# Row tiles in the plain aggregation runs: some gathers move from GpSimd to row-by-row DMAs of SyncE and ScalarE

## The reference

```python
h = layernorm(x + L0(x))       # messages (x @ weight[type])[src], summed by dst
h = layernorm(h + L1(h))       # mean of h[src] by dst, two 256x256 products, batch norm, relu
h = layernorm(h + L2(h))       # three attention layers: softmax by dst over the edges
h = layernorm(h + L3(h))       # (h @ W)[src] with degree norms, summed by dst
```

## Time and profile before

| | us |
|---|---|
| median of 3 runs | 6722.3 (6719.2 to 6724.4) |
| the profiled execution | 6704.8 |
| its span | 6703.0 |
| layer 0, to the first gather of a0 | 384.0 |
| POOL busy in the span | 4662.0 (70%) |
| PE busy | 4849.3 (72%) |
| DVE busy | 4466.5 (67%) |
| ACT busy | 2887.0 (43%) |

### The profile page before, as it was taken

The page is one execution under the profiler, slowest core; times in us unless marked ns, Lnnn a source line. Parts: engine busy times, 40 slices in busy tenths (PEclk is TensorE's granted clock), DMA queues, the critical chain, the costliest instruction groups (busy, mean ns, idle before and its releaser), DMA issues. The chain is left out here.

```text
span 6703.0 us, 99334 instructions
## 1 busy us (share of the span) xinstructions
PE 4849.3 (72%) x16858; PEld 2865.5 (43%) x16858; DVE 4466.5 (67%) x11760; ACT 2887.0 (43%) x11591; POOL 4662.0 (70%) x4938
## 2 busy tenths in 40 slices
PE   9977777777777757777675777775766777676666
PEld 4445555543444434444443444443444444333333
DVE  5145555555555578888886888886888888555554
ACT  3310000000000057888875888885788887000000
POOL 0057777767777727777776777777777777677776
PEclk9988778777777777878787888887787888767777
DMA  6444444433333345555544555555555553333333
GB/s 207 159 132 119 119 119 119 118 106 106 106 106 106 105 135 143 142 144 142 143 125 124 145 141 143 145 140 150 137 141 144 142 141 107 108 112 112 112 112 105
DMA packets 421891, 864.51 MB, mean 129 GB/s; under 512 B 103949, under 2 KB 246310, under 8 KB 421290
## 3 DMA queue, kind: packets, MB, share of 16 engines
q0 software_dynamic: 231040, 636.59, 34.6%
q1 hardware_dynamic: 151344, 184.21, 8.4%
q10 hardware_dynamic: 38906, 37.37, 1.8%
HBM read 755.70 MB, written 102.08 MB: 128 GB/s over the span
## 5 line engine op out<-in xcount | busy, mean ns | idle before, releaser
L631 POOL DMA_INDIRECT rows_a<-table,rows_src x2454 | 2348.8, 957 | 882.9 <-issue 527.3
L785 PE MATMUL ps<-rows_a,hot_a 128*128 x4980 | 1964.8, 513 | 749.6 <-DMA rows_a<-table,rows_tile_a 311.3
L1958 ACT ACTIVATE rows_a<-rows_a,ex_a 128x64 f32<-128x64 f32 x9588 | 2321.1, 337 | 0.0
L2035 PE MATMUL ps<-rows_a,hot_a 128*128 128x260 f32 x4908 | 1815.1, 490 | 161.0 <-DVE agg L1867 147.4
L729 DVE TENSOR_TENSOR agg<-agg,ps 128x256 f32 (+1 forms) x2490 | 1043.8, 419 | 1288.1 <-PE ps L785 1244.8
L686 POOL DMA_INDIRECT rows_a<-table,rows_tile_a x1500 | 1419.4, 946 | 456.9 <-issue 242.8
L785 PEld LDWEIGHTS ps<-rows_a,hot_a 128*128 128x128 f32 x4980 | 1059.2, 244 | 1574.8 <-DVE agg L729 824.7
L1867 DVE TENSOR_TENSOR agg<-agg,ps 128x260 f32 x2490 | 1037.6, 417 | 318.9 <-PE ps L2035 131.6
L2035 PEld LDWEIGHTS ps<-rows_a,hot_a 128*128 128x128 f32 x4908 | 973.7, 230 | 451.1 <-issue 346.3
L686 POOL DMA_INDIRECT rows_a<-table,row x782 | 742.3, 949 | 238.4 <-issue 140.0
L2125 ACT ACTIVATE root_a<-mv_a,eps 128x1 f32<-128x1 f32 x49 | 14.4, 295 | 973.5 <-DVE mv_a L2148 973.5
(11 more groups left out here) (341 smaller groups left out, 4223.8 us busy)
## 6 DMA issues: line engine op xcount, KB each, us to landing
dstt_a<-dloc_dram SPq DMA_DIRECT2D x156, 512.0 KB
own_a<-table SPq DMA_DIRECT2D x4608, 1.0 KB
table<-ob SPq DMA_DIRECT2D x48, 1024.0 KB, 4.4
rows_a<-table,rows_src POOLq DMA_INDIRECT x2454, 2.8
rows_a<-table,rows_tile_a POOLq DMA_INDIRECT x1500, 2.8
table<-ob_n SPq DMA_DIRECT2D x98, 130.0 KB, 2.8
rows_a<-table,row POOLq DMA_INDIRECT x782, 2.8
x_dram<-cur ACTq DMA_DIRECT2D x1, 6400.0 KB
```

Source lines behind the costliest of these rows:

```text
L631: nc.gpsimd.indirect_dma_start(out=rows[:, n % ring, 0:width], out_offset=None, in_=table, in_offset=bass.IndirectOffsetOnAxis(ap=index[:, ...
L785: nc.tensor.matmul(ps[n % banks][:, 0:width], hot[:, m % nbuf, j, :], mine[n % 4], start=True, stop=True).then_inc(step_done, 1)
L1958: ins = nc.scalar.mul(a, a, ex[:, k % GV, s, h:h + 1])
L2035: nc.tensor.matmul(ps[j % banks][:, 0:W4], hot[:, j, :], step_rows(k, j), start=True, stop=True).then_inc(step_done, 1)
```

## The change

Of the 782 tiles of each plain run, 29 are "row tiles", which POOL leaves out. Every 44th (43, 87, ... 747: 17 tiles) is fetched by SP row by row, 128 DMAs of 1024 bytes, with the row addresses loaded 32 at a time. Every 66th from 54 on (54, 120, ... 780: 12 tiles) is fetched by ACT in bursts of 16 rows: four bursts before its first block, then one inside each block's list and one behind it. The ring has 59 places instead of 64, and behind it lie three places for SP's tiles and two for ACT's, 64 in all. Layer 0 makes the places of these tiles and two lists of their row addresses, and stores the lists; SP loads a tile's list of 128 addresses before it or ACT asks for the rows. `AfterA1.act` and `AfterA5.act` get `between` behind their root in the same way as `AfterA0.act`.

```diff
-TRING = 64
+TRING = 59
 LOAD = 32
+OWN_TILE = 44
+OWN_TILES = tuple(range(OWN_TILE - 1, T - 1, OWN_TILE))
+OWN_PLACES = 3
+ACT_TILE = 66
+ACT_FIRST = 54
+ACT_TILES = tuple(range(ACT_FIRST, T - 1, ACT_TILE))
+ACT_PLACES = 2
+BURST = 16
+BURSTS_AHEAD = 4
...
@@ layer 0, SP behind L341 @@
+                        for q in range(2):
+                            sp.dma_start(own_tile_dram[q], own_tile[:, q]).then_inc(whole_out, 16)
@@ layer 0, DVE behind L449 @@
+                def own_place(stride, at, places, first):
+                    quotient(groups_of, tile, stride)
+                    ch.link(nc.vector.scalar_tensor_tensor(out=mine[:], in0=groups_of[:], scalar=float(-stride), in1=tile[:],
+                                                           op0=ALU.mult, op1=ALU.add))
...
+                own_place(OWN_TILE, OWN_TILE - 1, OWN_PLACES, TRING)
+                own_place(ACT_TILE, ACT_FIRST, ACT_PLACES, TRING + OWN_PLACES)
@@ aggregate, POOL @@
                 for t in range(T):
+                    if t in ROW_TILES:
+                        continue
@@ aggregate, SP @@
+                ask_index_of_act(0)
+                ask_index(0)
+                ask_index_of_act(1)
+                ready = 2
+                for i in range(len(OWN_TILES)):
+                    if i + 1 < len(OWN_TILES):
+                        ask_index(i + 1)
+                    if ready < len(ACT_TILES) and i == (ACT_TILE * ready - ACT_FIRST) // OWN_TILE:
+                        ask_index_of_act(ready)
+                        ready += 1
+                    if i >= OWN_PLACES:
+                        sp.wait_ge(step_done, min(OWN_TILES[i - OWN_PLACES] + NB, S))
+                    sp.wait_ge(own_in[i % 2], 16 * (i // 2 + 1))
+                    ask_rows(sp, mybir.EngineType.SP, own_index[:, i % 2], 0, P, LOAD, octets, 4 * D, table.shape[0] - 1,
+                             rows[:, TRING + i % OWN_PLACES, 0:D], own_full[i % OWN_PLACES])
@@ aggregate, ACT @@
+                def burst(done):
+                    q = next(bursts, None)
+                    if q is None:
+                        return
+                    i, lane = q * BURST // P, q * BURST % P
+                    place = i % ACT_PLACES
+                    if lane == 0:
+                        act.wait_ge(act_in[i % 2], 16 * (i // 2 + 1))
...
+                    ask_rows(act, mybir.EngineType.Activation, act_index[:, i % 2], lane, lane + BURST, BURST, octets, 4 * D,
+                             table.shape[0] - 1, rows[:, TRING + OWN_PLACES + place, 0:D], act_full[place])
+                    act.sem_inc(asked, 1)
+                for _ in range(BURSTS_AHEAD):
+                    burst(0)
                 for i in range(NB):
-                    after.act(act, i)
+                    after.act(act, i, lambda: burst(done_by(i)))
+                    burst(done_by(i))
@@ AfterA0.act @@
                 act.wait_ge(self.mixed, i + 1)
                 self.load_x(act, i + 2)
+            between()
             act.wait_ge(self.turned, i + 1)
```

More of the change, by code:

```diff
@@ L49 @@
 FW = 2 * P + 2
-TRING = 64
+TRING = 59
 LOAD = 32
+OWN_TILE = 44
[7 more added lines that the diff above has]
+BURSTS_AHEAD = 4
+assert not set(OWN_TILES) & set(ACT_TILES)
+ROW_TILES = (*OWN_TILES, *ACT_TILES)
+PLACES = OWN_PLACES + ACT_PLACES
 OWN_BATCH = 4
@@ L219, in steps_and_first_table @@
         odd = sb("odd", [P, SC], FP, c)
+        groups_of, mine, place = (sb(q, [P, SC], FP, c) for q in ("groups_of", "mine", "place"))
         joins = sb("joins", [P, 2, P], FP, c)
@@ L521, in _ @@
                                         4.0 * W4, None, ALU.mult)
+                for q, a in enumerate((row0, rows_tile)):
+                    for tiles, stride, lo in ((OWN_TILES, OWN_TILE, 0), (ACT_TILES, ACT_TILE, len(OWN_TILES))):
+                        n, at = len(tiles), tiles[0]
+                        each = a[:, 0:n * stride].rearrange("p (i e) -> p i e", e=stride)
+                        nc.vector.tensor_scalar(own_tile[:, q, lo:lo + n], each[:, :, at:at + 1].rearrange("p i e -> p (i e)"),
+                                                4.0 * D, None, ALU.mult)
                 nc.vector.tensor_copy(cont[:], crow.rearrange("o (k u) -> o u k", u=UG)[:, 0])
@@ L640, in build @@
     why_row = "row numbers are made from src and etype as the gathers' are"
-    why_slot = "slots are numbers modulo TRING"
+    why_slot = "slots are numbers modulo TRING, or one of the places behind the ring"
     def ask_rows(eng, of, numbers, lo, hi, load, flat, size, last, place, full):
@@ L645, in ask_rows @@
             _, at = nc.values_load_multi_w_load_instructions(
-                numbers[:, lane:lane + load], engines=[of], min_val=0, max_val=last * size,
+                numbers[:, lane:min(lane + load, hi)], engines=[of], min_val=0, max_val=last * size,
                 skip_runtime_bounds_check_because=why_row)
@@ L663, in aggregate @@
         width = D + 1 if with_deg else D
-        rows = sb(f"rows_{name}", [P, TRING, width], FP, c)
+        rows = sb(f"rows_{name}", [P, TRING + PLACES, width], FP, c)
+        own_index = sb(f"own_index_{name}", [1, 2, P], I32, c)
+        octets = table.bitcast(BYTE).rearrange("r b -> (r b)")
+        own_in = [sem(f"own_in_{name}{u}") for u in range(2)]
+        own_full = [sem(f"own_full_{name}{u}") for u in range(OWN_PLACES)]
+        act_index = sb(f"act_index_{name}", [1, 2, P], I32, c)
+        act_in = [sem(f"act_in_{name}{u}") for u in range(2)]
+        act_full = [sem(f"act_full_{name}{u}") for u in range(ACT_PLACES)]
+        asked = sem(f"asked_{name}")
         hot = sb(f"hot_{name}", [P, nbuf, u8, P], FP, c)
@@ L670, in aggregate @@
         for j in range(TRING):
-            used[j] += len(range(j, T, TRING))
+            used[j] += sum(1 for t in range(j, T, TRING) if t not in ROW_TILES)
         count = ps[7][:, 0:P]
@@ L697, in _, with ask_index, ask_index_of_act @@
                 after.sp_first(sp)
+                def ask_index(i):
+                    sp.dma_start(own_index[:, i % 2], own_tile_dram[0 if with_deg else 1, :, i:i + 1].rearrange("p o -> o p"),
+                                 allow_slow_non_contiguous=True).then_inc(own_in[i % 2], 16)
+                def ask_index_of_act(i):
+                    if i >= 2:
+                        sp.wait_ge(asked, P // BURST * (i - 1))
+                    at = len(OWN_TILES) + i
+                    sp.dma_start(act_index[:, i % 2], own_tile_dram[0 if with_deg else 1, :, at:at + 1].rearrange("p o -> o p"),
+                                 allow_slow_non_contiguous=True).then_inc(act_in[i % 2], 16)
+                ask_index_of_act(0)
[13 more added lines that the diff above has]
+                             rows[:, TRING + i % OWN_PLACES, 0:D], own_full[i % OWN_PLACES])
+                assert ready == len(ACT_TILES)
             @block.vector
@@ L747, in _ @@
                 after.act_first(act)
+                bursts = iter(range(len(ACT_TILES) * P // BURST))
+                def burst(done):
[6 more added lines that the diff above has]
+                        act.wait_ge(act_in[i % 2], 16 * (i // 2 + 1))
+                        if i >= ACT_PLACES:
+                            free = ACT_TILES[i - ACT_PLACES] + NB
+                            assert free <= done
+                            act.wait_ge(step_done, free)
+                    ask_rows(act, mybir.EngineType.Activation, act_index[:, i % 2], lane, lane + BURST, BURST, octets, 4 * D,
[3 more added lines that the diff above has]
+                    burst(0)
                 for i in range(NB):
-                    after.act(act, i)
+                    after.act(act, i, lambda: burst(done_by(i)))
+                    burst(done_by(i))
                 after.act_last(act)
+                assert next(bursts, None) is None
             @block.tensor
@@ L767, in rows_of @@
                     return views
-                landed, ahead = 0, rows_of(0)
+                landed, ahead, turns = 0, rows_of(0), list(base)
                 for m in range(UNITS):
@@ L781, in _ @@
                         while landed <= tile_by(n):
-                            u, turn = landed % TRING, landed // TRING
-                            pe.wait_ge(slot_full[u], 16 * (base[u] + turn + 1))
+                            if landed in OWN_TILES:
+                                w = OWN_TILES.index(landed)
+                                pe.wait_ge(own_full[w % OWN_PLACES], 16 * P * (w // OWN_PLACES + 1))
+                            elif landed in ACT_TILES:
+                                w = ACT_TILES.index(landed)
+                                pe.wait_ge(act_full[w % ACT_PLACES], 16 * P * (w // ACT_PLACES + 1))
+                            else:
+                                turns[landed % TRING] += 1
+                                pe.wait_ge(slot_full[landed % TRING], 16 * turns[landed % TRING])
                             landed += 1
```

(2 more changed lines are left out.)

16 lines of the change are left out of this document (13 added, 3 removed).

## The result

| | before | after |
|---|---|---|
| median us | 6723.2 (6719.2 to 6724.4, 4 runs) | 6894.8 (6888.1 to 6899.3, 4 runs) |
| ratio | | 1.0257, 95% interval 1.0245 to 1.0269 |
| span of the profiled execution | 6703.0 | 6886.0 |

What follows compares the result with a forecast made beforehand. POOL's time per gather was taken to bound the plain runs, ACT to become a0's bound. a1 -36, a5 -36, a0 +81 sum to +8 us: 6713 for the profiled execution, 6730 as median, range 6650 to 6800.

Steps and rivals of the forecast that it cites:

- What bounds, and POOL's share: Plain runs: POOL's time per gather sets the pace; 29 gathers left out save 36.3 us per run, 109 over three.
- SP step: SP fetching its 17 row tiles per run: it just keeps up with POOL, so no loss was taken.
- SP's tile: SP's row work: 52.1 us per tile, against 53.0 us POOL needs for 44 tiles.
- The slower rival: SP falls behind in a1 and a5 as two engines issuing make rows dearer, 55.5 us per tile; 6793 us, chance 0.23.
- a0: ACT's list becomes the bound there, 21.1 us per 16-step round; a0 loses 81 us instead of gaining 36.
- L868 starts no sooner than 9.15 us after the root: In a0, load_x and the first burst of 6.5 us delay ACT's copy of the turned block to 9.15 us.
- from L872 to L858 ... I take 2.4: In a0's round on ACT, the time from the product's copy to the copy of the next input: 2.4 us.
- a5: ACT's chain with both bursts takes 17.7 us and hides in 18.2; the run gains 36 us.
- 3.6 us from L2127's issue to L2130's end with the landing between: In a5, ACT's two stores, with the landing between them, take 3.6 us of its 17.7 us chain.
- Ring, places, layer 0: Ring of 59, extra copies and stores, and layer 0's 4.9 us of DVE work, taken as hidden: cost nothing.
- The rule on issuing engines: Spreading DMAs over issuing engines saves only issue time, usually small; by it a1 and a5 would gain nothing.
- The rival built on it: No gain from other queues: POOL's gathers lengthen by what they save, a0 loses; 6803 us, chance 0.05.

Runs made afterwards that it cites:

- x4_own: Changed kernel, but SP loads only ACT's first two address lists and ACT loads the others itself; 6890.2 us, ratio 1.0274 to the kernel before.
- x2_sp: Changed kernel with only SP's 17 tiles per run fetched by rows, ACT's 12 given back to POOL; 6648.3 us, ratio 0.9912 to the kernel before.
- x1_none: Changed kernel with all 29 row tiles given back to POOL, ring of 59, places and layer 0 lists kept; 6708.5 us, ratio 1.0002 to the kernel before.
- x3_act: Changed kernel with only ACT's 12 tiles per run fetched by rows, SP's 17 given back to POOL; 6823.3 us, ratio 1.0172 to the kernel before.
- x9_mid5: ACT loading its own later lists as in x4_own, a5's first burst moved between ACT's two stores; 6804.8 us, ratio 1.0143 to the kernel before.

## Why the prediction was wrong, step by step

- **What bounds, and POOL's share: right.** Gathers left out are worth 1.25 us each wherever POOL stays the bound: 17 to 21 us for 17 of them, 32 to 35 us in a1 for 29 (1055.6 and 1052.6 against 1087.7). The changed kernel got 28 there; the rest is SP's wait for `asked`, as x4_own shows, which the prediction's SP step left out.
- **SP's tile: right.** 52.1 us was said, 51.3 measured in x2_sp, and 50.6 to 51.5 in a1 of x4_own, beside ACT's rows. The slower rival had rows dearer by issue from two engines; SP's row takes 223 ns here, 228 in the earlier trace rows, so its mechanism is false. Its sign, PE waiting long for row tiles in a1 and a5 (239.0 and 111.5 us), came true for another reason, SP's wait for `asked`: without it the wait of the whole kernel falls from 376 to 93 us. What the rival had right is that the two streams meet; they meet in the landings.
- **a0: the mechanism was right, two terms too small.** "L868 starts no sooner than 9.15 us after the root" measured 9.82 (in the block shown, the burst with its load takes 6.76 us from the end of load_x, which itself ends 2.83 us after the root), and "from L872 to L858 ... I take 2.4" measured 3.22; the 2.4 came from two blocks of the earlier trace rows. 41 rounds of 16 steps x 1.5 us are 62 of the 69 us by which a0 was missed. Smaller terms make up the rest: the first root came 5 us later than said, the five rounds of 24 steps took 28.2 us instead of 26.3 and one early round 28.5, while the last two rounds, without bursts, took 23 us instead of 34.
- **a5: the failed step** is "3.6 us from L2127's issue to L2130's end with the landing between", taken from a run without row DMAs and costed as hidden with 0.5 us to spare. With the landing, the second store started 4.8 us behind the first instead of 3.1, and the load of addresses behind the second store, priced at 1.2, took 2.6: ACT's list is 21.5 us, not 17.7. ACT alone, with 2.6 us from store to store and 2.3 for that load, has 18.9 and loses little by it (-10 us where 15 were to be had, x3_act), so the landing beside both streams is the main part. From -36 to +61, this step is 97 of the 175 us between the forecast of the profiled execution's span (8 us over the kernel before) and the measured one (183 over it); a0 is 69.
- **Ring, places, layer 0: right,** nothing (x1_none; layer 0 is 1.3 us longer).
- **The rule on issuing engines** (the Trainium skill, "DMA: Bandwidth & Descriptors", section "Issuing engines are not separate DMA queues"). Rows first: a1 gains 28 to 35 us, so issue time is worth having, and by the rule as I had read it a1 would have stayed. The rival built on it, in which POOL's gathers lengthen by what they save, is false here: they take 946 ns in the median before and after. But the rule's first half, that all DMAs end on the same engines and interleave, fits what a5 shows: 4.8 us from store to store with both streams, 2.6 and 2.9 with one.

## What to carry to other kernels

A piece of work moved into an in-order engine's list costs what the list's next consumer waits, so look for the place where the list waits for something long (a landing, another engine's steps) and put the piece there: with SP's rows beside them, the same 16 rows cost a5 88 us more ahead of the first store than between the two, and there ACT's 12 tiles gained their full 12 us (962.7 against 974.8 in x2_sp). A landing measured without row DMAs is no price for it when two engines issue them. And a long wait in the trace (239 us of PE in a1 for row tiles, 20 in x4_own) costs only what the following steps can't catch up, 2 to 7 us there.

## What was new about the hardware

- Single-row DMAs of SP and ACT pass one at a time. From 1560 to 2470 us of the changed kernel 3,632 row packets of 1024 bytes moved; none began more than 8 ns before the one before it ended, though they come from two engines' queues, while of the 34,610 packets of POOL's queue (gathered rows and 4-byte ones) 27,825 overlapped the one before. The Trainium skill, "DMA: Bandwidth & Descriptors", section "Why a DMA increments its semaphore by 16 and not by 1", says that a DMA issued from SP or ACT which is split over k of the 16 DMA engines takes the lowest-numbered k; it doesn't name the k of a single row. Each row is one packet here, and if every row went to the same engine, "one at a time" would follow; the trace agrees with that, and doesn't tell which engine.
- A row takes 46 ns in the median to move, and rows are issued 0.32 us apart, yet up to 8 of SP's and 5 of ACT's rows (95th percentiles) wait when both issue. Whether the gathers' packets on the same engine make the difference was not tried.
- A load of 16 addresses takes 1.0 to 1.4 us in a0, in a1 and behind a5's root, but 2.0 to 2.8 us right behind a5's second store, with SP's rows (2.56 in the median) and without them (2.28). In x9_mid5, where 16 rows stand between the two stores, it takes 1.2 to 2.7 there (1.92 in the median). The cause stays open.
